# Second attention of a four-stage kernel: full-array operations at four places a batch, two casts moved from GpSimd to ScalarE

## The reference

```python
h = _layernorm(x, g, b)
kv = h @ W_kv
qk, v = jnp.split(kv, 2, axis=-1)          # 16 heads of 8 features each
scores = jnp.einsum('bhqd,bhkd->bhqk', qk, qk)
a1 = jax.nn.softmax(scores, axis=-1)
a1 = jnp.einsum('gh,bhqk->bgqk', W_x, a1)  # mixes the heads
o1 = jnp.einsum('bhij,bhjd->bhid', a1, v)
return o1.transpose(0, 2, 1, 3).reshape(b, n, dims) @ W_out
```

## Time and profile before

| | us |
|---|---|
| median of 3 executions | 1669.99 (1667.52 to 1671.85) |
| profiled execution, its own time | 1660.28 |
| its span in the profile | 1658.4 |
| second attention with all engines in steady state | about 780 to 1475 |
| one batch there | 23.16 and 23.25 in turn |

### The profile page before, as it was taken

How to read it: one execution, slowest core, us unless ns; L and a number is a source line. 1 busy time by engine, 2 the same in 40 slices (tenths; PEclk the granted TensorE clock), 3 DMA queues, 4 the chain that set the end, 5 groups by cost and what they waited for, 6 DMA issues and landing times. The chain is left out here.

```text
span 1658.4 us, 56350 instructions
## 1 busy us (share of the span) xinstructions
PE 1571.1 (95%) x17756; PEld 1120.3 (68%) x17756; DVE 1269.6 (77%) x3471; ACT 1062.7 (64%) x2468; POOL 967.8 (58%) x1129
## 2 busy tenths in 40 slices
PE   4999999999999889988999999999999999998998
PEld 3344444444444367765888888888888888887997
DVE  5778888888878479977777777777877777773666
ACT  0567777777777656763676666676676667774332
POOL 4445454544443045556877887778877788762222
PEclk7899999999999899997999999999999999999999
DMA  7333333333333100012222222222222222200111
GB/s 208 101 103 106 105 102 114 101 106 104 105 100 98 34 23 28 28 46 85 82 79 64 73 80 79 75 65 70 83 75 68 71 75 83 69 31 14 63 63 54
DMA packets 170167, 129.07 MB, mean 78 GB/s; under 512 B 13036, under 2 KB 143224, under 8 KB 170104
## 3 DMA queue, kind: packets, MB, share of 16 engines
q1 hardware_dynamic: 169136, 127.65, 24.9%
q10 hardware_dynamic: 968, 0.60, 0.1%
HBM read 60.56 MB, written 54.53 MB: 69 GB/s over the span
## 5 line engine op out<-in xcount | busy, mean ns | idle before, releaser
L817 DVE TENSOR_REDUCE shifts<-bank 128x2 bf16<-128x512 f32 x1024 | 693.2, 692 | 159.8 <-PE bank L972 146.0
L767 ACT ACTIVATE probs<-bank 128x512 f32<-128x512 f32 x1024 | 588.6, 594 | 156.6 <-PE bank L965 143.3
L911 PE MATMUL bank<-values,probs 64*128 64x129 f32 x8192 | 576.8, 279 | 0.7 <-DVE o_even L785 0.6
L911 PEld LDWEIGHTS bank<-values,probs 64*128 64x128 f32 x8192 | 508.7, 188 | 51.7 <-issue 26.8
L965 PE MATMUL bank<-q_stack,k_stack 49*128 49x256 bf16 x2048 | 384.8, 276 | 38.0 <-DMA q_stack<-shift_rows 27.9
L972 PE MATMUL bank<-k_stack,q_stack 48*128 48x256 bf16 x2048 | 388.7, 280 | 11.6 <-DMA q_stack<-score_parts 7.4
L593 POOL TENSOR_TENSOR values<-mix,v_in 128x1024 f32<-128x1024 f32 x128 | 301.3, 2364 | 3.0 <-ACT v_in L733 3.0
L965 PEld LDWEIGHTS bank<-q_stack,k_stack 49*128 49x128 bf16 x2048 | 145.2, 95 | 181.9 <-issue 76.7
L602 POOL TENSOR_TENSOR o_odd<-o_odd,scaled 128x256 f32<-128x256 f32 x224 | 162.9, 727 | 148.4 <-ACT scaled L697 148.4
L697 ACT ACTIVATE scaled<-bank,recips 128x128 f32<-128x128 f32 x448 | 139.2, 362 | 111.0 <-DVE recips L811 109.8
L902 PE MATMUL bank<-probs,values 128*32 128x256 f32 x2048 | 170.4, 406 | 0.0
(11 more groups left out here) (146 smaller groups left out, 2159.9 us busy)
## 6 DMA issues: line engine op xcount, KB each, us to landing
score_parts<-parts SPq DMA_DIRECT2D x128, 192.0 KB, 2.3
k_stack<-score_parts SPq DMA_DIRECT2D x256, 96.0 KB
q_stack<-score_parts SPq DMA_DIRECT2D x256, 96.0 KB
score_parts<-parts SPq DMA_DIRECT2D x128, 128.0 KB, 2.2
score_parts<-parts SPq DMA_DIRECT2D x128, 64.0 KB, 1.8
x_in_f<-x_all SPq DMA_DIRECT2D x64, 128.0 KB, 2.0
x_in<-in_L_attn_x SPq DMA_DIRECT2D x32, 128.0 KB, 3.1
q_stack<-shift_rows SPq DMA_DIRECT2D x256, 2.0 KB
```

Source lines behind the costliest of these rows:

```text
L767: act.activation(probs[:, s % RING, :, :].rearrange("p t n -> p (t n)"), s2[s % 2][:, :], ACT.Exp, scale=scale).then_inc(exp_done, 1)
L817: dve.tensor_reduce(shifts[:, :, hf, col], s1[s % 2][:, :].rearrange("p (t n) -> p t n", t=TILES), op=ALU.max, axis=AX.X, negate=True).the ...
L911: return pe.matmul(pv_bank(h)[:, q * (D + 1):(q + 1) * (D + 1)], probs[rows, h % RING, t, q * P:(q + 1) * P], values[b.odd][rows, t, h, :] ...
```

## The change

In the second attention the seven places with full-array operations become four: step 1 (second half of the shifts, then qk, now of batch `i + 2`), step 9 (first half of the shifts, then `ot`), step 11 (`out`), step 13 (`v`, now of batch `i + 2`, then `xt`). The shifts are padded with zeros to 128 columns, so that their transposes load 128 weight columns instead of 8. `v` and the shifts get columns of their own in the shared bank. The row-paired matmuls are now written one by one, each with its own waits in front: the wait for the maxima stands between the first second-score and the first first-score matmul, and the wait for `half_done` stands behind the first lower product. Of the four operations of the qk split, the two that only cast go from GpSimd to ScalarE: `parts[0]` is a second copy from PSUM at step 1, `parts[1]` is made at step 4 (`second_part`), and the last subtraction (`last_part`) is on GpSimd at step 5, behind a multiplication of the values. On ScalarE the normalisation (`norm`) moves behind the exponential of step 15, and `v_in` is taken at step 15. The first attention runs the same functions in its old order of operations, with the wait for the maxima between its score matmuls too.

```diff
-        self.shifts0 = 11 if first else 12
-        self.v = 14 if first else 2
+        self.shifts0 = 11 if first else 9
+        self.v, self.v_ahead = (14, 1) if first else (13, 2)
         self.xt = 0 if first else 13
-        self.q = 3 if first else 15
+        self.q, self.q_ahead = (3, 3) if first else (1, 2)
...
-        self.ot = 11 if first else 8
-        self.out = 13 if first else 10
+        self.ot = 11 if first else 9
+        self.out = 13 if first else 11
...
-    shifts = sb("shifts", [P, TILES, 2, half_heads], BF16)
+    shifts = sb("shifts", [P, TILES, 2, half_heads if first else P], BF16)
...
+                if s == 5 and on(slots.split):
+                    last_part(i.plus(slots.split))
                 if s in (4, 6, 8, 10) and on(1):
                     mix_values(i, (s - 4) // 4, s // 2 % 2)
...
+            if not first:
+                pool.wait_ge(part0_ready, times(b, 0, n))
+                wait(pool, part1_ready, times(b, -1, n))
+                pool.tensor_tensor(rest[:, :, :], exact[:, :, :], parts[:, 0, :, :], op=ALU.subtract).then_inc(rest_ready, 1)
+                return
...
+        def last_part(b):
+
+            if not first:
+                pool.wait_ge(part1_ready, times(b, 0, n))
             pool.tensor_tensor(parts[:, 2, :, :], rest[:, :, :], parts[:, 1, :, :], op=ALU.subtract).then_inc(parts_ready, 1)
...
+        def take_qk(b):
+
+            act.wait_ge(qk_in_psum, times(b, 0, n))
+
+            wait(act, rest_ready, times(b, -1, n))
             act.activation(exact[:, 0, :], m1[:, 0:TOK], ACT.Copy).then_inc(qk_taken, 1)
+            wait(act, parts_written, times(b, -1, n) * (32 * len(RUNS)))
+            act.activation(parts[:, 0, 0, :], m1[:, 0:TOK], ACT.Copy).then_inc(part0_ready, 1)
+
+        def second_part(b):
+
+            act.wait_ge(rest_ready, times(b, 0, n))
+            act.activation(parts[:, 1, 0, :], rest[:, 0, :], ACT.Copy).then_inc(part1_ready, 1)
 
         def step(i, on):
             for s in range(HEADS):
+                if not first and s == slots.q and on(slots.q_ahead):
+                    take_qk(i.plus(slots.q_ahead))
+                if not first and s == 4 and on(slots.q_ahead):
+                    second_part(i.plus(slots.q_ahead))
                 if s == slots.shifts1 and on(0):
                     shift_rows_out(i, 1)
...
+                if not first and s == 15 and on(slots.v_ahead):
+                    act.wait_ge(v_in_psum, times(i, slots.v_ahead, n))
+
+                    wait(act, values_ready, times(i, 1, n) * (2 * TILES))
+                    act.activation(v_in[:, :, :].rearrange("p t d -> p (t d)"), m0[:, TOK:2 * TOK], ACT.Copy).then_inc(v_taken, 1)
...
+        def lower_product(b, h, k):
+
+            if k == 0:
+                if h == 0:
+                    pe.wait_ge(values_ready, (b.number() + 1) * (2 * TILES))
+                pe.wait_ge(exp_done, b.number() * HEADS + (h + 1))
...
+            product = half_of_products(b, h, 0, k)
+            if k == TILES * TILES - 1:
+                product.then_inc(half_done, 1)
+
+        def upper_product(b, h, k):
+
+            if k == 0:
+                pe.wait_ge(half_done, b.number() * HEADS + (h + 1))
+            product = half_of_products(b, h, 1, k)
+            if k == TILES * TILES - 1:
+                product.then_inc(pv_done, 1)
...
+            for t in range(TILES):
+                score(s % 2, t)
+                score(1 - s % 2, t)
+            for k in range(TILES * TILES):
+                lower(k)
+                upper(k)
```

More of the change, by code:

```diff
@@ L35 @@
 BESIDE = 2
+SHIFTS_AT = 2 * TOK
 class Slots:
@@ L755, in step @@
                     scale_head(i if s > 4 else i.plus(-1), (s - 4) % HEADS)
-                if not first and s == slots.q and on(3):
-                    take_qk(i)
-                if not first and s == slots.norm and on(-1):
-                    norm(i.plus(-1))
                 if on(0):
@@ L768, in step @@
                                    scale=scale).then_inc(exp_done, 1)
+                if not first and s == slots.norm and on(-1):
+                    norm(i.plus(-1))
         return step
@@ L868, in step @@
                                           rstd[:, t:t + 1], ALU.subtract, ALU.mult).then_inc(x_ready, 1)
+        if not first:
+            dve.memset(shifts[:, :, :, half_heads:P], 0.0).then_inc(ones_ready, 1)
         for v in values:
@@ new lines, in upper_product, with second_score @@
+        def upper_product(b, h, k):
[4 more added lines that the diff above has]
+                product.then_inc(pv_done, 1)
+        def second_score(b, s, t):
+            if t == 0:
+                if s % half_heads == 0:
+                    pe.wait_ge(shifted[s // half_heads], b.number() * 32 + 32)
+                wait(pe, exp_done, b.number() * HEADS + (s - 1))
+            rows = stack_rows(s % 2, HEAD_ROWS + 1)
+            score = pe.matmul(s2[s % 2][:, t * TOK:(t + 1) * TOK], core.k_stack[b.odd][rows, s // 2, t * P:(t + 1) * P],
+                              core.q_stack[b.odd][rows, s // 2, :], start=True, stop=True)
+            if t == TILES - 1:
+                score.then_inc(s_in_psum, 1)
@@ L959, in scores, with both_scores @@
                 wait(pe, max_done, b.number() * HEADS + (s - 1))
+            h = s ^ 1
+            rows = stack_rows(h % 2)
+            score = pe.matmul(s1[s % 2][:, t * TOK:(t + 1) * TOK], core.q_stack[b.odd][rows, h // 2, t * P:(t + 1) * P],
+                              core.k_stack[b.odd][rows, h // 2, :], start=True, stop=True)
+            if t == TILES - 1:
+                score.then_inc(max_in_psum, 1)
+        def both_scores(i, on, s):
             for t in range(TILES):
-                tile = slice(t * P, (t + 1) * P)
@@ L963, in scores @@
                 if on(0):
[L964 to L975 removed]
+                    second_score(i, s, t)
@@ L1052, in step @@
-                if s == slots.xt and on(3):
-                    b = i.plus(3)
-                    pe.wait_ge(x_loaded[b.odd], (b.half + 1) * 16)
-                    wait(pe, y_ready, times(i, -2 if first else -1, n))
-                    wait(pe, qk_taken, times(i, 2, n) * sides)
-                    if not first and on(1):
-                        pe.wait_ge(shift_rows_ready, i.plus(1).number() * 2 + 1)
-                    for t in range(TILES):
-                        last = pe.transpose(m1[:, t * P:(t + 1) * P], x_in[b.odd][:, t, :], core.ident[:, :])
-                    last.then_inc(xt_in_psum, 1)
@@ L1064, in step @@
-                if s in (slots.q, slots.k) and on(3):
-                    b = i.plus(3)
-                    side = int(s == slots.k)
-                    if side == 0:
-                        pe.wait_ge(xt_ready, times(i, 3, n))
-                    else:
-                        wait(pe, shift_rows_ready, times(i, 0, n) * 2)
-                        wait(pe, v_taken, times(i, 0, n))
-                        wait(pe, qk_taken, times(i, 2, n) * 2)
-                    if first:
-                        for v in range(2):
-                            last = pe.matmul((m1, m0)[side][:, v * TOK:(v + 1) * TOK], core.w0_qk[:, side, v, :],
-                                             x_t[b.odd][:, :], start=True, stop=True)
-                    else:
-                        last = pe.matmul(m1[:, 0:TOK], core.w1_qk[:, :], x_t[b.odd][:, :], start=True, stop=True)
-                    last.then_inc(qk_in_psum, 1)
```

294 lines of the change are left out of this document (162 added, 132 removed).

## The result

The changed kernel takes 1642.85 us (median of 4 executions, 1639.43 to 1647.88) against 1670.78 (1667.52 to 1671.85) for the kernel before: ratio 0.984, 95% interval 0.982 to 0.987. The forecast was 1645. The profiled execution took 1647.88 us, with a span of 1646.1 and a granted clock of 0.953.

A forecast was written before the change was run, and what follows sets the result against it. TensorE's own stream was taken to bound each 23.25 us batch; gathering (0.24) and moved waits (net 0.72) less 0.10 for ScalarE give 22.39, 26 us over 30 batches, 1 back: 1645 us from 1670, range 1626 to 1664.

The forecast's parts named there:

- the moved wait is the larger part: TensorE, second attention: half_done wait behind the first lower product saves 0.84 us a batch, net 0.72, against 0.24 for gathering.
- two signs by which it would be wrong: TensorE in the changed profile: plain steps differing from 1.20 us, or waits above 0.3 us a batch.
- A plain step of 1.21, never under 1.20: TensorE's plain steps fall from 1.28 to 1.21 us; the lower half loses 0.09 of the old 0.16.
- Both readings: TensorE plain steps: weights queue behind waiting ones, 1.21 us; or they pass, 1.12 and 1.28 in turn, 1.20 on average.
- The rival that both halves run free: TensorE: 1.12 us in all twelve plain steps, 57 us less, 1613 us; chance 0.08.
- Gathering gives 0.24: TensorE, second attention: seven full-array places made four, alone, shorten a batch from 23.25 to 23.01 us.
- The stretches: TensorE, first small matmul to first score at steps 1, 9, 11, 13: 0.74, 0.49, 0.64, 0.82 us, together 2.69.
- ScalarE late by 0.1 at step 3, behind an exponential: ScalarE's filled step 1 delays TensorE's second-score weights at step 3: 0.10 us a batch, bounds 0 and 0.3.
- ScalarE's full steps bind: Rival: exponentials of steps 1 and 9 come 0.2 to 0.3 us later, 15 us lost, 1657 to 1660 us; chance 0.12.
- Parts 3.7 us later, no stall: GpSimd and SyncE: first parts write at 1008.6 instead of 1004.84; shift rows 0 late, 0.2 us the other end.
- The rival on the slow side: Shift rows late through last_part and SyncE; each us late costs one a batch at step 0, 1680 us at 1.2; chance 0.07.

The follow-up runs named there:

- waits_old: Changed kernel with its four places, but the second attention's product and score waits together again as in the kernel before: ratio 0.999 to the kernel before, 1659.5 us.
- split_only: Kernel before with its seven places, only the second attention's product and score waits moved: ratio 0.976 to the kernel before, 1621.4 us.
- scale_first: Changed kernel with ScalarE's scaling of the odd head put ahead of the copies in odd steps: ratio 0.979 to the kernel before, 1622.0 us.
- act_extra: Changed kernel with one more, unused copy of qk on ScalarE at step 1: ratio 0.987 to the kernel before, 1640.2 us.
- narrow_shifts: Changed kernel with the shifts' transposes at 8 columns again, not padded to 128: ratio 0.987 to the kernel before, 1637.9 us.
- extra_wait: Changed kernel with one more, already met wait ahead of each lower product of the second attention: ratio 0.979 to the kernel before, 1628.5 us.
- products_old: Changed kernel with only the products' waits put together again, the scores' waits staying apart: ratio 1.001 to the kernel before, 1665.5 us.

## Why the prediction was right, and where it was not

The time came out right, 1643 for 1645, and so did the reason that was put first, that the moved wait is the larger part. The steps inside it erred on both sides and made up for each other, so that a hit within 2 us is in good part luck. The prediction named two signs by which it would be wrong, plain steps other than 1.20 and waits of TensorE above 0.3 us a batch, and both came. A batch of 22.39 was forecast and 22.17 measured:

| a batch, us | forecast | measured |
|---|---|---|
| twelve plain steps, nothing waiting | 15.04 - 0.84 = 14.20 | 12 x 1.116 = 13.39 |
| four places with the rest of their steps | 7.97 + 0.12 = 8.09 | 7.98 |
| stands, most of them for ScalarE | 0.10 | 0.80 |

- *A plain step of 1.21, never under 1.20.* This step failed. It held that the second lower product's weights stand behind the upper ones that wait, or that odd steps make good what even ones gain. Both readings gave 1.20 because both took TensorE's order of issue to be its order of starting. The rows at 1104.14 and 1104.24 show otherwise. The page TensorE: Matmul & The Clock Gate of the Trainium skill, in Part 3 under The mechanism, has matmuls start in strict program order; this trace does not agree, by 0.10 us between the two halves. The rival that both halves run free (0.08) had the mechanism and was put too low; its time, 1613, was missed for want of the waits below. The upper half still comes to `half_done` 0.33 us behind the start of the last lower product (single records of the trace: the product at 1104.03, the upper weights at 1104.36), but that is just when its own turn is, since it trails by 0.10 all the time, and the lower half's second weights load 0.01 later, in their own turn as well.
- *Gathering gives 0.24.* On TensorE alone the sum is sound: `waits_old` without its stand at step 2 would be at 23.03. With the halves free each place saved is worth more, since no place hides a wait any longer: twelve free steps and four places would be 21.37, against 22.11 for `split_only`. The waits take it back.
- *The stretches* 0.74, 0.49, 0.64, 0.82: measured 0.71, 0.45, 0.64, 0.86.
- *ScalarE late by 0.1 at step 3, behind an exponential.* This step failed too, in place and size. The prediction added up ScalarE's step 1 in the right order (scaling behind three copies), a little long: on average over 24 batches the exponential ends 1.98 us behind the first score, not 2.25, and 0.51 ahead of the load that needs it. It then followed only the exponential to its user. The scaling has one too, the lower products one step on, because it gives back their bank. The rival *ScalarE's full steps bind* had about the right price, 15 us (0.45 x 30 = 14 by `scale_first`), but by the exponential again.
- *A chain that was not in the sum*: steps 8 and 0, where the bank comes back some 0.15 and 0.21 us later than a stream without stands asks for it. With plain steps of 1.28 it is hidden (`waits_old`, step 8: 1.277), with 1.115 it shows. The 0.80 in the table is all stands together, these two included.
- *Parts 3.7 us later, no stall.* First write 2.04 us behind the products of step 3 before, 5.97 after (1102.13 to 1108.10): 3.9 later, and from 830 us on the shift rows stop TensorE once, 0.2 us. That the chain has 0 to 1 us to spare was right too. In `scale_first` it binds: the qk copies stand behind the scaling there, so that the shift rows go out 6.43 us behind the products of step 9 for 6.13 in the changed kernel (averages over 27 batches), and the batch is shorter besides. The same wait comes up in two or three batches of `act_extra`, `narrow_shifts` and `extra_wait` too. The rival on the slow side described the chain well and put its price too high.
- *30 full batches, 1 us back, first attention 0.* 33.0 us came out of the second attention for 30 x 1.04 = 31 in the batches. The profiled execution missed its own forecast, 1647.9 for 1635, by a first attention of 560 us at a granted clock of 0.95, where its partner had 0.97. Outside the two attentions the profiles have some 378 us before and 380 after, so that the 1 us back is neither shown nor refuted.

## What to carry to other kernels

Where an engine issues work for two independent halves, put each wait directly ahead of the instruction that needs it: doing this for the products and the scores was worth 2.4% here, with everything else left alone, and without it for the products (`waits_old`, `products_old`) nothing was gained. After every gain of this kind, list each buffer's return path (who frees the bank, and what is queued in front of it) against the new length of a step, since chains that fitted into 1.28 us don't fit into 1.12. When full steps are gathered, order each engine's work in them by who is waited for next, not by who comes ready first.

## What the runs showed of the hardware

- Matmuls of the two 64-row halves start out of the order of issue, by 0.10 us, and each half goes on at 0.11 us a record. A wait that isn't met does hold up both halves: at the stand of step 2 no upper product starts ahead of the lower ones at 1123.09, though its own count was raised by a product that started at 1122.45; with the 0.33 us measured above it would have been seen at about 1122.78 (an estimate).
- A wait for a count already reached costs nothing in a plain step of TensorE's stream: sixteen more a batch, plain steps unchanged at 1.115 us.
- Transposes that load 8 columns between full-width matmuls cost 0.13 us more than the same padded to 128.
- The first attention of the same code took 540 to 561 us, by a granted clock of 0.98 to 0.95 over it; a difference of 1.3% of the run that no line of code accounts for.
